# Merging the narrow jobs of the hyperbolic heads in a two-layer transformer: four heads in one job instead of two

## The reference

```python
tq = jnp.sqrt(1.0 / curv + jnp.sum(q * q, axis=-1, keepdims=True))
tk = jnp.sqrt(1.0 / curv + jnp.sum(k * k, axis=-1, keepdims=True))
inner = jnp.einsum('bhtd,bhsd->bhts', q, k) - tq * jnp.swapaxes(tk, -1, -2)
arg = jnp.maximum(-curv * inner, 1.0 + 1e-07)
dis = jnp.sqrt(1.0 / curv) * jnp.arccosh(arg)
scores = 1.0 / (eps + dis) + causal_bias
out = softmax(scores) @ v
```

## Time and profile before

| | us |
|---|---|
| median of 3 runs | 2564.33 |
| lowest, highest | 2559.43, 3105.05 |
| the profiled execution, device time | 2583.99 |
| its span, first to last instruction | 2582.2 |

### The profile page before, as it was taken

One profiled execution on the slowest core, in us unless ns is written; L12 is line 12 of the kernel. 1 busy time (PEld: TensorE's weight loads), 2 busy tenths in 40 slices (PEclk: granted clock), 3 DMA queues, 4 the chain that ended last, 5 costly groups with the idle time before them and its releaser, 6 DMA issues. The chain is left out here.

```text
span 2582.2 us, 30828 instructions
## 1 busy us (share of the span) xinstructions
PE 2217.8 (86%) x11109; PEld 873.0 (34%) x11109; DVE 1486.7 (58%) x3043; ACT 1343.8 (52%) x1923; POOL 833.9 (32%) x909
## 2 busy tenths in 40 slices
PE   6799976779999998778999999777899999877789
PEld 2233432234433342223443344222343334322243
DVE  6562556856556266675656445677565635577552
ACT  2345447962244635795225553688423454378922
POOL 1112125533411313562331221365142122146534
PEclk7899977879999986588999998767899999766889
DMA  5200231004310023100520022110051002401013
GB/s 145 67 15 18 67 99 36 1 1 119 101 28 2 21 78 83 36 1 13 143 72 20 2 66 80 36 36 1 23 156 42 20 2 83 98 9 27 1 53 88
DMA packets 67850, 128.38 MB, mean 50 GB/s; under 512 B 11397, under 2 KB 24837, under 8 KB 63077
## 3 DMA queue, kind: packets, MB, share of 16 engines
q1 hardware_dynamic: 67696, 126.40, 17.9%
HBM read 109.99 MB, written 15.20 MB: 48 GB/s over the span
## 5 line engine op out<-in xcount | busy, mean ns | idle before, releaser
L1281 DVE TENSOR_REDUCE mx<-ps 128x1 f32<-128x512 f32 (+3 forms) x992 | 612.5, 655 | 373.8 <-PE ps L620 241.3
L1029 ACT ACTIVATE pr<-ps 128x1024 f32<-128x1024 f32 (+3 forms) x672 | 515.0, 804 | 404.3 <-PE ps L690 403.7
L690 PE MATMUL ps<-qop,kop 75*128 75x512 bf16 (+7 forms) x1344 | 407.6, 367 | 123.1 <-DVE wb L1343 41.5
L617 PE MATMUL ps<-kop,qop 72*128 72x512 bf16 (+6 forms) x1248 | 425.4, 374 | 92.1 <-DVE mx L1281 69.7
L1572 POOL TENSOR_SCALAR_AFFINE_SELECT pr<-pr 128x512 f32<-128x512 f32 x224 | 145.5, 649 | 730.9 <-ACT pr L1029 730.1
L736 PE MATMUL ps<-pr,vt 128*32 128x512 f32 (+3 forms) x2688 | 340.4, 584 | 8.2 <-POOL pr L1572 7.6
L1090 ACT ACTIVATE pr<-ps 128x512 f32<-128x512 f32 x224 | 133.8, 597 | 337.6 <-PE ps L846 273.7
L617 PEld LDWEIGHTS ps<-kop,qop 72*128 72x128 bf16 (+1 forms) x1248 | 128.1, 105 | 424.9 <-DVE mx L1281 256.1
L690 PEld LDWEIGHTS ps<-qop,kop 75*128 75x128 bf16 (+1 forms) x1344 | 121.6, 104 | 361.7 <-ACT pr L1029 117.9
L856 PE MATMUL ps<-pr,w_down 128*128 128x512 f32 x384 | 196.7, 599 | 4.1 <-POOL pr L1563 4.1
L843 PE MATMUL ps<-hT,w_gate 128*128 128x512 f32 x384 | 196.2, 592 | 0.2 <-DVE on L1508 0.2
(11 more groups left out here) (316 smaller groups left out, 3153.0 us busy)
## 6 DMA issues: line engine op xcount, KB each, us to landing
wb<-gates_scratch SPq DMA_DIRECT2D x192, 256.0 KB, 3.4
kop<-kparts_scratch SPq DMA_DIRECT2D x32, 576.0 KB
qop<-qparts_scratch SPq DMA_DIRECT2D x96, 192.0 KB
on<-hmax_scratch SPq DMA_DIRECT2D x8, 1024.0 KB, 5.7
kparts_scratch<-on SPq DMA_DIRECT2D x12, 256.0 KB, 2.9
qparts_scratch<-on SPq DMA_DIRECT2D x12, 256.0 KB, 4.9
qparts_scratch<-wb SPq DMA_DIRECT2D x12, 192.0 KB
kparts_scratch<-wb SPq DMA_DIRECT2D x12, 192.0 KB
```

The lines of the kernel that those rows point to most:

```text
L617: mm = pe.matmul(o, qop[0:k, slot(l, u), j, qb * P:(qb + 1) * P], kop[0:k, slot(l, u), j, k0:k0 + wd], start=True, stop=not diag)
L690: mm = pe.matmul(o, kop[0:k, slot(l, u), 2 * pair + j, kb * P:(kb + 1) * P], qop[0:k, slot(l, u), 2 * pair + j, q0:q0 + wd], start=True, s ...
L1029: nc.scalar.activation(pr[:, g % 3, 2 * pair:2 * pair + 2, o0:o0 + wd], ps[:, bank:bank + 2, o0:o0 + wd], ACT.Exp).then_inc(a.exps, 1)
L1281: ins_ = nc.vector.tensor_reduce(mx[:, nth(l, u) % 2, j0:j0 + heads, qb, col % 2], ps[:, bank, 0:heads * wd].rearrange("p (j n) -> p j n", ...
```

## The change

Steps with at most 256 columns become one job with all four heads; steps with 512 or 384 columns keep their two jobs of two heads. `HYP_JOBS` lists the jobs as pairs of a step and its heads: six in chunk 0 and fourteen in chunk 1, 20 in place of 24. They start at positions 1 to 6 and 9 to 22; chunk 1 thus begins at position 9, as before. A job of four heads is as wide as a job of two heads of twice the columns: two heads side by side in each of the two banks and in each half of `hyp_x` and `hyp_z`. Elementwise instructions take the job whole (1024 columns for a step of 256, 512 for one of 128), POOL's scaling and PE's matmuls still go by head. The tiles are used from their first column on, where before they were used at the columns of the step. The outputs of the hyperbolic unit are copied out at 11 and 27, before at 13 and 29.

```diff
+HYP_JOBS = [(i, heads) for i, x in enumerate(STEPS)
+            for heads in (((0, 1), (2, 3)) if x[3] > CH // 2 else ((0, 1, 2, 3),))]
 def hyp_diagonals(k):
-    return sum(STEPS[i // 2][4] for i in range(k))
+    return sum(STEPS[i][4] for i, _ in HYP_JOBS[:k])
+def hyp_jobs_until(step):
+    return sum(i < step for i, _ in HYP_JOBS)
+def hyp_lines(k):
+    return sum(len(heads) for _, heads in HYP_JOBS[:k])
+def hyp_width(k):
+    i, heads = HYP_JOBS[k]
+    return STEPS[i][3] * len(heads) // 2
+def hyp_head(z, k, j):
+    wd = STEPS[HYP_JOBS[k][0]][3]
+    n = len(HYP_JOBS[k][1]) // 2
+    return z[:, j // n, j % n * wd:(j % n + 1) * wd]
...
-HYP_HALVES = 2 * NS
-HYP_POS = [1 + k for k in range(HYP_HALVES)]
+HYP_POS = [1 + k + 2 * (STEPS[i][0] > 0) for k, (i, _) in enumerate(HYP_JOBS)]
...
-        outs += [(HYP_POS[2 * (4 + 8 * c) - 1] + 5, HYP_UNIT, c) for c in range(NC)]
+        outs += [(HYP_POS[hyp_jobs_until(4 + 8 * c) - 1] + 5, HYP_UNIT, c) for c in range(NC)]
...
-            return z[:, :, q0 - c * CH:q0 - c * CH + wd]
+            return z[:, :, 0:hyp_width(k)]
+        def hyp_bank(bank, k):
+            i, heads = HYP_JOBS[k]
+            o0 = STEPS[i][2] % CH if len(heads) == 2 else 0
+            return ps[:, bank:bank + 2, o0:o0 + hyp_width(k)]
...
-                    for j in range(2):
-                        mm = pe.matmul(ps[:, bank + j, o0:o0 + wd],
-                                       kop[0:K_HYP, slot(l, HYP_UNIT), 2 * (k % 2) + j, kb * P:(kb + 1) * P],
-                                       qop[0:K_HYP, slot(l, HYP_UNIT), 2 * (k % 2) + j, q0:q0 + wd],
+                    for j, head in enumerate(heads):
+                        mm = pe.matmul(hyp_head(hyp_bank(bank, k), k, j),
+                                       kop[0:K_HYP, slot(l, HYP_UNIT), head, kb * P:(kb + 1) * P],
+                                       qop[0:K_HYP, slot(l, HYP_UNIT), head, q0:q0 + wd],
                                        start=True, stop=True)
...
-                    for i in range(2):
-                        j = 2 * (k % 2) + i
+                    for i, j in enumerate(heads):
                         h = 4 * HYP_UNIT + j
                         mm = pe.matmul(ps[32 * j:32 * j + 32, 5, o0:o0 + wd], vt[:, kb, 32 * h:32 * h + 32],
-                                       z[:, i], start=kb == 0, stop=kb == 4 * c + 3, tile_position=(0, 32 * j))
+                                       hyp_head(z, k, i), start=kb == 0, stop=kb == 4 * c + 3,
+                                       tile_position=(0, 32 * j))
...
-                    nc.vector.tensor_scalar(hyp_x(k), ps[:, bank:bank + 2, o0:o0 + wd], -1.0, ARG_GAP, ALU.mult,
+                    nc.vector.tensor_scalar(hyp_x(k), hyp_bank(bank, k), -1.0, ARG_GAP, ALU.mult,
...
+                    if len(heads) == 4:
+                        z = z.rearrange("p a (j n) -> p a j n", j=2)
+                        least = least.rearrange("p (a j) n -> p a j n", j=2)
...
-                    nc.vector.tensor_tensor(z, z, nbc[:, j0:j0 + 2, q0:q0 + wd], ALU.add).then_inc(h_sub, 1)
+                    nc.vector.tensor_tensor(z, z, least, ALU.add).then_inc(h_sub, 1)
...
-                    for i in range(2):
-                        j = 2 * (k % 2) + i
-                        z = hyp_z(b, k)[:, i]
+                    for i, j in enumerate(HYP_JOBS[k][1]):
+                        z = hyp_head(hyp_z(b, k), k, i)
                         nc.gpsimd.tensor_scalar(z, z, hyp[:, 4 + j:5 + j], HYP_EPS, ALU.mult, ALU.add).then_inc(h_lin, 1)
```

More of the change, by code:

```diff
@@ L385, in hyp_x @@
         def hyp_x(k):
-            c, _, q0, wd, _ = STEPS[k // 2]
-            return wb[:, 0, 2 * (k % 2):2 * (k % 2) + 2, q0 - c * CH:q0 - c * CH + wd]
+            return wb[:, 0, 2 * (k % 2):2 * (k % 2) + 2, 0:hyp_width(k)]
         def hyp_z(b, k):
-            c, _, q0, wd, _ = STEPS[k // 2]
             z = (hT(b).rearrange("p (j n) -> p j n", j=2), tmp.rearrange("p (j n) -> p j n", j=2), rsb[:],
                  wb[:, 1, 0:2], wb[:, 1, 2:4])[k % HYP_RING]
-            return z[:, :, q0 - c * CH:q0 - c * CH + wd]
+            return z[:, :, 0:hyp_width(k)]
[3 more added lines that the diff above has]
+            return ps[:, bank:bank + 2, o0:o0 + hyp_width(k)]
         fa, fh = pr[:, 1, 0:3], pr[:, 2, 0:3]
@@ L698, in hyp_scores @@
                 def hyp_scores(k):
-                    c, kb, q0, wd, diag = STEPS[k // 2]
-                    o0 = q0 - c * CH
+                    step, heads = HYP_JOBS[k]
+                    c, kb, q0, wd, diag = STEPS[step]
                     if k == 0:
@@ L754, in hyp_values @@
                         pe.wait_ge(h_exp, k + 1)
-                    if kb == 0 and c and k % 2 == 0:
+                    if kb == 0 and c and heads[0] == 0:
                         pe.wait_ge(a.o_out, out_before(HYP_UNIT, c))
                     z = hyp_z(b, k)
-                    for i in range(2):
-                        j = 2 * (k % 2) + i
+                    for i, j in enumerate(heads):
                         h = 4 * HYP_UNIT + j
                         mm = pe.matmul(ps[32 * j:32 * j + 32, 5, o0:o0 + wd], vt[:, kb, 32 * h:32 * h + 32],
-                                       z[:, i], start=kb == 0, stop=kb == 4 * c + 3, tile_position=(0, 32 * j))
+                                       hyp_head(z, k, i), start=kb == 0, stop=kb == 4 * c + 3,
+                                       tile_position=(0, 32 * j))
                     mm.then_inc(h_pv, 1)
@@ L1010, in hyp_score @@
                     z = hyp_z(b, k)
-                    act.wait_ge(h_lin, 2 * (k + 1))
+                    act.wait_ge(h_lin, hyp_lines(k + 1))
                     link(nc.scalar.activation(z, z, ACT.Ln))
@@ L1324, in outputs_out @@
                     if is_hyp(l, u):
-                        dve.wait_ge(h_pv, 2 * (4 + 8 * c))
+                        dve.wait_ge(h_pv, hyp_jobs_until(4 + 8 * c))
                     else:
@@ L1335, in hyp_arg @@
                 def hyp_arg(k):
-                    c, kb, q0, wd, _ = STEPS[k // 2]
-                    o0 = q0 - c * CH
                     bank = 2 * (JOBS[l].index((True, k, k % 2)) % 2)
@@ L1351, in hyp_shift @@
                 def hyp_shift(k):
-                    c, kb, q0, wd, _ = STEPS[k // 2]
-                    z, j0 = hyp_z(b, k), 2 * (k % 2)
+                    step, heads = HYP_JOBS[k]
+                    c, kb, q0, wd, _ = STEPS[step]
+                    z, least = hyp_z(b, k), nbc[:, heads[0]:heads[-1] + 1, q0:q0 + wd]
+                    if len(heads) == 4:
+                        z = z.rearrange("p a (j n) -> p a j n", j=2)
+                        least = least.rearrange("p (a j) n -> p a j n", j=2)
                     dve.wait_ge(hm_in[c], 16)
                     dve.wait_ge(h_score, k + 1)
-                    nc.vector.tensor_tensor(z, z, nbc[:, j0:j0 + 2, q0:q0 + wd], ALU.add).then_inc(h_sub, 1)
+                    nc.vector.tensor_tensor(z, z, least, ALU.add).then_inc(h_sub, 1)
                 if l == 0:
@@ L1575, in hyp_cut @@
             def hyp_cut(k):
-                if STEPS[k // 2][4]:
-                    past = hyp_z(b, k)[:, :, 0:P]
+                step, heads = HYP_JOBS[k]
+                if STEPS[step][4]:
+                    past, same = hyp_z(b, k)[:, :, 0:P], [[0, 2]]
+                    if len(heads) == 4:
+                        past = hyp_z(b, k).rearrange("p a (j n) -> p a j n", j=2)[:, :, :, 0:P]
+                        same = [[0, 2], [0, 2]]
                     pool.wait_ge(h_exp, k + 1)
-                    nc.gpsimd.affine_select(past, past, [[0, 2], [1, P]], ALU.is_ge, 0.0, base=0,
+                    nc.gpsimd.affine_select(past, past, same + [[1, P]], ALU.is_ge, 0.0, base=0,
                                             channel_multiplier=-1).then_inc(h_cut, 1)
```

## The result

The changed kernel takes 2581.49 us (median of 4 runs), the kernel before 2562.63 us in the same session. The ratio is 1.007, with a 95% interval of 1.0038 to 1.0101: slower by about 19 us. That is inside the range and under the 2% that a measurement tells from no change by itself, but it isn't the +0.4 us that was forecast. It is the number of rival B (2580).

The account below looks back on a forecast made before the run. ACT, 81% busy, was taken as the busiest engine in layer 1's four attention loops, though not last everywhere. Front -6.0 and tail +6.4 us gave +0.4 on the median 2564.33: 2564.7, say 2565; range 2546 to 2583.

Parts of the forecast that it names:

- rival B: Attention loops: wide jobs ready later on DVE where ACT has run dry, nothing returned elsewhere; +15.6 us, 2580; chance 0.20.
- ACT, 16 us less: Four attention loops: sixteen merges each save about 1.0 us of ACT, 16 us at most from ACT alone.
- PE, about 0.8 off per merge: Value matmuls on PE: four heads side by side save the second half job's turn, about 0.8 us a merge.
- Positions 9 and 10, -2.3 a batch: Front: position 9's job comes earlier as PE and DVE lose work before it; -2.3 us, bounds 0 and 4.9.
- Position 22, +1.9: Tail: ACT waits 1.06 us longer for the job, then roots 0.85 longer; +1.9 us in each batch.
- 24: Position 24: statistics stand behind the shift awaiting the wider score; 0, +1.4, +0.9, +0.2 us in batches 0 to 3.
- 25: Position 25, same chain as the position before: +0.4 us, in batch 3 -0.5.
- Position 6, +1.0: Front: ACT's square root grows by 0.85 us and DVE reaches the maxima 1.06 later; +1.0 us a batch.
- Position 7: 0; its chain is pieces and maxima: Front: no change, since the job started at 6 is again 512 wide and ACT's larger log hides in its wait.
- Positions 14 to 21, nothing: Middle of the loop: no change forecast, 0 us; jobs at 9 to 20 keep their place and size.
- Positions 26 to 29, -1.4: End of the loop: PE, the full engine, loses two sets of values; -1.4 us a batch, -1.8 in batch 3.
- Rival C: The granted clock falls otherwise, moving the sum 5 to 8 us either way, the change's own effect nil; chance 0.07.

Follow-up runs that it names:

- e8: Changed kernel with argument, root and addition of the 256-column four-head jobs done by halves, each with its own signal; 2589.70 us, ratio 1.010.
- e3: Changed kernel with the hyperbolic unit's output and turn two positions later, at 13 and 29; 2588.38 us, ratio 1.0092.
- e9: Changed kernel with the first chunk's four-head jobs one position later, at 6 and 7; 2582.40 us, ratio 1.0089.
- e11: Kernel with only the 128-column steps merged, its hyperbolic output and turn moved one position later; 2563.86 us, ratio 1.002.
- e7: Changed kernel with POOL's addition of a four-head job split into two instructions, one signal after the second; 2585.70 us, ratio 1.009.
- e12: Changed kernel with a wait meant to delay POOL's addition; it held nothing back, so a repeat of the changed kernel; 2582.11 us, ratio 1.0087.

## Why the prediction was wrong, and where it was right

The outcome lies in the range, but only as the range was wide enough to hold rival B; the forecast itself, +0.4 us, missed the +19 us. By its steps:

- *ACT, 16 us less.* Nearly right: 13.8 less busy, 0.86 a merge in place of 1.0, and the five lines of root, score and last exponential together have 400 records. A wide root is 1051 to 1057 ns, a log 1133 to 1138, as in the earlier trace rows.
- *PE, about 0.8 off per merge.* The values of the hyperbolic jobs fell from 115.5 to 111.2 us, -4.3 in place of -10; 64% of their records ran at half clock, before 55%.
- *Positions 9 and 10, -2.3 a batch.* Right in sign and about in size: -1.3, -2.6, -1.5 and -2.6; the 11.7 us named for batch 0 were 12.73.
- *Position 22, +1.9.* Right: +1.9, +2.1, +2.5, +2.5; *24*: 0, +1.4, +0.9, +0.1, and *25*: +0.4 in three batches, within a tenth. The wait grew as forecast. The Trainium skill's advice to break instructions up where their bubbles hold others (Perfetto Trace Analysis, Optimizing Scalar/DVE Operations) agrees with the trace so far as whole jobs go (position 22 is at 6.4 to 7.0 us with half jobs, 8.3 to 9.0 with wide ones), and so far as the wait goes within a wide job (e8: about 1.1 us less). In time neither that nor anything else of e8 paid.
- *Position 6, +1.0, and "Position 7: 0; its chain is pieces and maxima".* This is the step that failed: +4.0 forecast over the batches, +13.4 measured (+9.2 at 6, +4.2 at 7). The wide job's time on DVE was charged to ACT's wait only. It also stands ahead of the reduction for which PE's last piece waits, and PE's queue carries that into position 7's pieces, whose chain I had right but whose start I took as fixed. The forecast also had nothing for DVE being held beside POOL's wider addition (2.3 us in two of four batches), nor for the values at half clock.
- *Positions 14 to 21, nothing.* +4.1. That the output comes at 11 and no longer at 13 was known; the step left out is where its turn lands. Positions 14 and 15 cost 8.4 more, and 16 to 21 give 4.3 back.
- *Positions 26 to 29, -1.4.* -2.9 in all of 26 to 35 in place of -6.0. Batches 1 to 3 gave 0.8, 1.9 and 1.2; batch 0 lost 0.9, its 26 to 29 at a granted clock of 0.50 (10.90 to 11.49 us), where 0.69 had been granted.
- *Rival C.* Its size (5 to 8 us) is right for one stretch, and its statement that the change's own effect is nil is wrong. It isn't an alternative to B. In the repairs e3, e9 and e11 the stretch 17 to 19 got longer at a lower clock (from 0.85 to 0.97 down to 0.75 or 0.76 in eight of the twelve batches), which goes with C; that the clock is the cause there wasn't tested.

B's condition was that the wait at 21 passes 1.5 us and 9 and 10 stay over 13.5. The first held (1.86), the second didn't (12.73). B reached +15.6 by striking out the gains at 9, 10 and 26 to 29, 15.2 us. Measured, 9 and 10 gave 7.9 of their 9.2 us, and 9.4 more than forecast was lost at 6 and 7 and 4.1 in the middle. That B's 2580 stands next to the measured 2581.49 is luck.

What stays open: what brings the granted clock down in positions 15 to 19, and how the loss at 6 and 7 divides between the late argument, the half clock and the stall (by e7 the stall's part could be some 3 to 5 us over the four batches, an estimate from 95.9 us there against 99.2 and 101.0 in the changed kernel and its repeat e12).

## What to carry to other kernels

Merging two instructions to save their fixed cost pays where the merged one is small, and turns round once it holds an in-order engine longer than the slack of whoever is queued behind it: here jobs of 512 columns made of two of 256 gained 7 us (ratio 0.9973), and jobs of 1024 made of two of 512 lost 13 (1.0054). Before costing a wider instruction, follow not only its consumer but the next instruction on its own engine, and the buffer that that one frees, and look at what another engine's longer instruction can hold up. When a table of equal positions shows the same work at two lengths, read the clock column before crediting a repair to the edit.

## What the runs showed of the hardware

- A DVE operation of 128x16 beside a POOL addition ends when the POOL instruction ends: 2.29 us beside 2.35, 1.22 and 1.19 beside two of 1.27, against 0.17 alone. A reduction from PSUM (L1312, two of 256 columns) beside the same addition takes 0.43 us in batch 0 of e12, as without it. The Trainium skill (SBUF — State Buffer, Who interferes with whom) describes this: the port pair shared by the two engines is an exclusive lock for the whole instruction. The trace agrees, and shows that 16 columns are enough to be held. The page adds that the one issued first holds the pair. In the stalls of 2.27 to 2.32 us in the changed kernel and in e12 POOL had begun first, by 0.06 to 0.10 us. The other way round, in batch 1 of the kernel before, an addition of 512 columns that began 0.07 us after the shift L1356 took 2.00 us in place of 1.27.
- Tenths of a us decide whether the stall comes: in the changed kernel DVE's L1250 started 0.09 us after the addition in batches 2 and 3 (stall) and 0.65 us before it in batch 0 (no stall).
- The same six jobs in positions 17 to 19 took 23.65 us at a granted clock of 0.97 and 27.94 at 0.68, but also 23.65 at 0.86.
